# Masked maxima of an attention layer: ScalarE puts the mask into PSUM, and VectorE's mask and norm work is reordered

## What is computed

```
query = _layernorm(q @ Wq + bq, qn_scale, qn_bias)
key = _layernorm(kv @ Wk + bk, kn_scale, kn_bias)
...
scores = jnp.einsum('bhqd,bhkd->bhqk', query, key) / jnp.sqrt(jnp.asarray(D_K, query.dtype))
m = mask[:, None, :, :]
scores = jnp.where(m == 0, NEG_INF, scores)
probs = jax.nn.softmax(scores, axis=-1)
out = jnp.einsum('bhqk,bhkd->bhqd', probs, value)
...
x = x + jnp.tanh(g_xattn[1]) * _L1_xattn_ref(ctx_1024, _layernorm(x, axis=-1), mask_BxSxS2_ik0, ...)
```

## Time and profile before

| | us |
|---|---|
| median of 3 runs | 2475.44 (2474.05 to 2477.65) |
| span of the profiled execution, first to last instruction | 2475.2 |
| TensorE busy in it | 2414.1 |
| VectorE busy | 1444.5 |
| ScalarE busy | 1087.0 |

### The profile page before, as it was taken

How to read it: one execution, slowest core, us unless ns; L and a number is a source line. 1 busy time by engine, 2 the same in 40 slices (tenths; PEclk the granted TensorE clock), 3 DMA queues, 4 the chain that set the end, 5 groups by cost and what they waited for, 6 DMA issues and landing times.

```text
span 2475.2 us, 33128 instructions
## 1 busy us (share of the span) xinstructions
PE 2414.1 (98%) x13344; PEld 1826.1 (74%) x13344; DVE 1444.5 (58%) x2410; ACT 1087.0 (44%) x1762; POOL 245.9 (10%) x223
## 2 busy tenths in 40 slices
PE   6999999999999999999989999999999999999998
PEld 5666667688888888888755666666778888888886
DVE  5555566542222222222666666665888888888986
ACT  4343433442222222223334333334666666666665
POOL 2021112210000000000301111112000000000000
PEclk9999999999999999999999999999999999999999
DMA  3121111421101100102311222223501101101000
GB/s 126 35 86 52 52 52 69 158 85 52 52 1 52 51 18 35 51 18 85 113 58 61 78 78 78 78 73 102 167 18 35 52 18 48 38 20 49 35 30 22
DMA packets 92600, 147.27 MB, mean 59 GB/s; under 512 B 5408, under 2 KB 28320, under 8 KB 92448
## 3 DMA queue, kind: packets, MB, share of 16 engines
q1 hardware_dynamic: 92448, 145.16, 17.4%
HBM read 111.59 MB, written 33.55 MB: 59 GB/s over the span
## 4 chain that ended last, share of the span: by engine, by line
PE 40%; DVE 8%; ACT 2%; issue 1%; DMA 0%; POOL 0%; SPq 0%; DVEq 0%; ACTq 0%
PE l_lay_bank L69 18%; PE l_lay_score L69 11%; PE l_lay_values L1493 1%; PE l_lay_score L1416 1%; PE l_lay_score L1418 1%; PE l_lay_score L1468 1%; PE l_lay_values L1497 1%; PE l_lay_sums L1505 1%; DVE l_at_at_next L1036 1%; DVE l_at_h_lo L1050 1%; DVE l_at_at_next L1029 1%; DVE l_at_full L1025 1%; DVE l_at_full L1018 1%; DVE l_at_xTf_lo L924 1%; PE l_lay_bank L1339 1%
## 5 line engine op out<-in xcount | busy, mean ns | idle before, releaser
L69 PE MATMUL l_lay_score<-l_at_tw_hi,l_at_h_hi 128*128 128x512 f32 x1024 | 401.5, 392 | 5.2 <-DVE l_at_h_lo L1050 4.7
L69 PE MATMUL l_lay_bank<-l_at_xTf_hi,l_at_tw_hi 128*128 128x512 f32 x1024 | 400.0, 391 | 0.0
L69 PE MATMUL l_lay_score<-l_at_tw_hi,l_at_h_lo 128*128 128x512 f32 x1024 | 398.7, 389 | 0.0
L69 PE MATMUL l_lay_score<-l_at_tw_lo,l_at_h_hi 128*128 128x512 f32 x1024 | 398.5, 389 | 0.0
L69 PE MATMUL l_lay_bank<-l_at_xTf_hi,l_at_tw_lo 128*128 128x512 f32 x1024 | 398.4, 389 | 0.0
L69 PE MATMUL l_lay_bank<-l_at_xTf_lo,l_at_tw_hi 128*128 128x512 f32 x1024 | 398.4, 389 | 0.0
L1010 DVE TENSOR_TENSOR l_at_h_lo<-l_at_full,l_at_h_hi 128x512 fp32r<-128x512 f32 x128 | 99.6, 779 | 466.0 <-ACT l_at_h_hi L740 466.0
L735 ACT ACTIVATE l_at_full<-l_lay_bank,l_at_lay_b 128x512 f32<-128x512 f32 x128 | 88.4, 690 | 457.5 <-PE l_lay_bank L69 457.5
L69 PEld LDWEIGHTS l_lay_score<-l_at_tw_hi,l_at_h_hi 128*128 128x128 f32 x1024 | 192.2, 188 | 49.2 <-DVE l_at_h_lo L1050 10.3
L69 PEld LDWEIGHTS l_lay_score<-l_at_tw_hi,l_at_h_lo 128*128 128x128 f32 x1024 | 192.2, 188 | 40.3
L69 PEld LDWEIGHTS l_lay_bank<-l_at_xTf_hi,l_at_tw_lo 128*128 128x128 f32 x1024 | 192.2, 188 | 40.0
(11 more groups left out here) (224 smaller groups left out, 4078.9 us busy)
## 6 DMA issues: line engine op xcount, KB each, us to landing
both_x_in<-stream SPq DMA_DIRECT2D x25, 1024.0 KB, 5.6
l_at_xg<-stream SPq DMA_DIRECT2D x23, 1024.0 KB, 5.5
stream<-l_at_xg SPq DMA_DIRECT2D x22, 1024.0 KB, 4.3
l_at_tw_raw<-in_l_w SPq DMA_DIRECT2D x64, 256.0 KB, 5.6
l_at_maskT_in<-in_maskT SPq DMA_DIRECT2D x40, 256.0 KB, 2.6
both_x_in<-in_x SPq DMA_DIRECT2D x9, 1024.0 KB, 7.6
l_at_xg<-in_x SPq DMA_DIRECT2D x7, 1024.0 KB, 5.3
out<-l_at_xg SPq DMA_DIRECT2D x7, 1024.0 KB, 4.3
```

The source lines that it names most:

```text
L69: done = nc.tensor.matmul(out, lhs[a], rhs[b], start=first and n == 0, stop=last and n == len(passes) - 1)
```

## The change

ScalarE writes the mask into PSUM for maxima 4 to 15 of chunks 1 to 7 of layer 1 (`seed_max`), and TensorE's key product accumulates onto it. Maxima 0 to 3 and all of chunk 0 keep the identity product. From maximum 4 on three pairs of banks rotate, `values` and `sums` being the third. `seed_max` stands on ScalarE behind `s_evict`; its first one waits for `c_out` and `s_out`, the others for the reduction of maximum m - 3. On VectorE the four main pieces of the transposed mask move from among the maxima of chunk `it` to the start of the next turn of the loop, `mask_front` and x's norm move ahead, and one query piece moves. On SyncE pieces 3 and 4 are loaded at the head of the turn in which they are used.

```diff
@@ PSUM and the rotation
-        score = n.ps("score", [P, GH, 512])
-        values = n.ps("values", [P, 512])
-        sums = n.ps("sums", [P, 512])
+        score = n.ps("score", [P, GH + 2, 512])
+        values, sums = score[:, GH, :], score[:, GH + 1, :]
+        SEED0 = 4
+        N_SEED = NM - SEED0
+        pair_of = lambda it, m: m % 2 if it == 0 or m < SEED0 else (m - 2) % 3
+        pair_before = lambda m: m - 3 if m > SEED0 else None
+        max_banks = lambda it, m: score[:, 2 * pair_of(it, m):2 * pair_of(it, m) + 2, 0:2 * KEYS]
@@ SyncE, the loop over chunks
             for it in range(NCH):
+                if norm and it:
+                    load_maskT(it, 3)
+                    load_maskT(it, 4)
                 if it < last:
                     load(it + 2)
                 else:
                     load_last_residual()
-                if norm and it + 2 < NCH:
-                    load_masks(it + 2)
+                if norm and it:
+                    load_maskT(it + 1, 0)
+                    load_maskT(it + 1, 1)
                 if norm:
-                    for i in range(2, PIECES):
-                        load_maskT(it + 1, i)
-                    load_maskT(it + 2, 0)
-                    load_maskT(it + 2, 1)
+                    if it + 2 < NCH:
+                        load_masks(it + 2)
+                    load_maskT(it + 1, 2)
@@ ScalarE
+            def seed_max(it, m):
+                if m == SEED0:
+                    act.wait_ge(mask_done, it + 1)
+                    act.wait_ge(c_out, KT * it)
+                    act.wait_ge(s_out, it)
+                else:
+                    act.wait_ge(max_done, NM * it + pair_before(m) + 1)
+                nc.scalar.activation(max_banks(it, m).rearrange("p a (h k) -> p a h k", h=2),
+                                     mask_add[:, m % QT, :].unsqueeze(1).unsqueeze(1)
+                                     .broadcast_to([P, 2, 2, KEYS]), ACT.Copy).then_inc(seeded, 1)
...
                 s_evict(it)
+                if more and norm:
+                    for m in range(SEED0, NM):
+                        seed_max(it + 1, m)
@@ VectorE, the loop over chunks
-                xT_front(it + 1)
+                xT_front(it + 1, (0, 1))
+                if norm and it:
+                    maskT_front(it, 1)
+                    maskT_front(it, 2)
+                xT_front(it + 1, (2, 3))
...
                 if norm:
+                    if it:
+                        maskT_front(it, 3)
+                        maskT_front(it, 4)
+                    mask_front(it + 1)
+                    q_rows_front(it + 1, (0, 1))
+                    maskT_front(it + 1, 0)
+                    norm_stats(it + 2)
+                    q_rows_front(it + 1, (2,))
+                    norm_apply(it + 2)
+                    q_rows_front(it + 1, (3,))
                     q_norm_stats(it + 1)
+                    q_norm_apply(it + 1)
...
                 for m in range(NM):
                     max_of(it + 1, m)
-                    if m in (2, 3) and norm:
-                        qT_front(it + 1, (m,))
-                    if m in (4, 6, 10, 13) and norm:
-                        maskT_front(it + 1, {4: 1, 6: 2, 10: 3, 13: 4}[m])
+                    if m in (1, 3, 5) and norm:
+                        qT_front(it + 1, ((m + 1) // 2,))
@@ TensorE, max_of
-                if m >= 2:
+                if seed:
+                    pe.wait_ge(seeded, N_SEED * (it - 1) + m - SEED0 + 1)
+                elif m >= 2:
                     pe.wait_ge(max_done, NM * it + m - 1)
...
-                    if norm:
+                    if norm and not seed:
                         nc.tensor.matmul(to, ident_bf[:, :], mask_add[:, q, :].unsqueeze(1)
                                          .broadcast_to([P, 2, KEYS]), start=True, stop=False)
                     done = nc.tensor.matmul(to, qT_of(it)[0][:, t, q * P:(q + 1) * P],
                                             keys.bd[:, b, t, 2 * a:2 * a + 2, :],
-                                            start=not norm, stop=True)
+                                            start=not norm, stop=True, skip_group_check=seed)
```

More of the change, by code:

```diff
@@ L590, in _ @@
                     add_bias(last, gate_bias)
+                if it < last:
+                    x_rstd_of(it + 2)
                 if norm and it < last:
                     q_rstd_of(it + 1)
-                if it < last:
-                    x_rstd_of(it + 2)
                 if it:
@@ L967, in max_of @@
                 dve.wait_ge(max_ps, NM * it + m + 1)
-                heads = score[:, 2 * (m % 2):2 * (m % 2) + 2, 0:2 * KEYS]\
-                    .rearrange("p a (h k) -> p a h k", h=2)
+                heads = max_banks(it if norm else 0, m).rearrange("p a (h k) -> p a h k", h=2)
                 to = maxes[:, q, :].rearrange("p (j c) -> p j c", c=DH)[:, :, t]
@@ L1189, in _ @@
                     k_lo_of(1)
-                for half in ((0, 1), (2, 3)):
-                    if norm:
[L1192 to L1196, removed]
-                if norm:
+                if norm:
+                    if it:
[8 more added lines that the diff above has]
+                    q_rows_front(it + 1, (3,))
                     q_norm_stats(it + 1)
-                    norm_stats(it + 2)
                     q_norm_apply(it + 1)
                 else:
+                    q_front(it + 1, (0, 1))
+                    norm_stats(it + 2)
+                    q_front(it + 1, (2, 3))
                     norm_apply(it + 2)
@@ L1205, in _ @@
                 if norm:
-                    mask_front(it + 1)
-                    maskT_front(it + 1, 0)
-                    norm_apply(it + 2)
-                    qT_front(it + 1, (0, 1))
+                    qT_front(it + 1, (0,))
                 if it:
@@ L1226, in _ @@
                     front.take_lo(dve, "wd")
-            xT_front(NCH)
+            xT_front(NCH, (0, 1))
+            if norm:
+                maskT_front(last, 1)
+                maskT_front(last, 2)
+            xT_front(NCH, (2, 3))
             recip_of(last - 1)
+            if norm:
+                maskT_front(last, 3)
+                maskT_front(last, 4)
             for u in range(2):
@@ L1400, in max_of @@
                 t, q, b = m // QT, m % QT, it // CPB
+                seed = norm and it > 0 and m >= SEED0
                 if m == 0 and norm:
@@ L1413, in max_of @@
                 for a in range(2):
-                    to = score[:, 2 * (m % 2) + a, 0:2 * KEYS].rearrange("p (h k) -> p h k", h=2)
-                    if norm:
+                    to = max_banks(it if norm else 0, m)[:, a, :].rearrange("p (h k) -> p h k", h=2)
+                    if norm and not seed:
                         nc.tensor.matmul(to, ident_bf[:, :], mask_add[:, q, :].unsqueeze(1)
```

1 line of the change is left out of this document (added).

## The result

The changed kernel takes 2523.22 us (2522.25 to 2528.7, 4 runs), the kernel before on the same chip 2474.74 us (2473.79 to 2477.65, 4 runs). The ratio is 1.0194, with a 95% interval of 1.0181 to 1.0207: slower, by 48.5 us, where 5.2 had been forecast. The profiled execution has a span of 2526.9 us.

The account below looks back on a forecast made before the run. TensorE's own work was taken to bound the maxima of chunks 2 to 7. Maxima -14.3, late mask pieces +11.2 (chunks 2 to 7) and +5.9 (chunk 1), clock +2.4: +5.2 us, giving 2480.6 us; range 2468 to 2489.

Parts of the forecast that it names:

- the train and its feeder: Maxima 4 to 15, chunks 2 to 7: 0.98 us a step, ScalarE's mask 0.7 us, 1.1 us lost before maximum 4.
- the new order: Norm work reordered on VectorE and GpSimd: fills VectorE's own gaps, put at 0.
- The term of -14.3 us: Maxima of chunks 2 to 7: 3.5 us won less 1.1 lost in each of six chunks, 14.3 us gained.
- the landing: Mask pieces 3 and 4 behind the residual's load: land 7.1 us after its issue, TensorE goes on after 7.6.
- the stores: Stores ahead of the residual's load: 4.36 us each gives 9.6 us of stops, this trace's durations 13.0; 11.2 taken.
- I take 7.1: Time from the large load's issue until a mask piece behind it lands: 7.1 us, bounded below by 3.6.
- the forecast's faster rival: Mask pieces ready 4.1 us after the residual's issue; only chunk 1 stops, for 2.4 us; -12 us, 2463.5; chance 0.16.
- Its conversion, 0.42 us: VectorE's conversion of a late mask piece before the scores' mask products: 0.42 us, within the 7.6 until TensorE goes on.
- one fall for sure and half of another: 2.4 us: TensorE's clock behind the stops: one certain fall of 1.7 us and half of another, 2.4 us in all.
- a stop of 1.6 us is probably free of it: TensorE's clock: probably no fall after a 1.6 us stop; 5.9 us is not free, 3 us may not be.
- Chunk 1, put at 0: Chunk 1's maxima: no gain or loss, 0 (-1 to +1), the 2.3 us loop being as long as its three reductions.

Follow-up runs that it names:

- e8: Kernel before with only the changed order of norm, mask and qT on VectorE and of rstd on GpSimd; no ScalarE masks, mask pieces unmoved: 2477.08 us.
- e4: Changed kernel plus one wait: GpSimd's addition of the gate's bias starts only after VectorE has converted the chunk's mask pieces: 2493.48 us.
- e9: Changed kernel with mask pieces 3 and 4, from the second chunk on, converted by ScalarE and not VectorE; GpSimd's addition unchanged: 2494.18 us.
- e6: Changed kernel with unread products added on TensorE just ahead of the products that wait for the mask pieces, filling the stops: 2513.32 us.
- e1: Changed kernel with the mask pieces' loads and conversions back in their old places; ScalarE's masks and the new order kept: 2465.95 us.
- e2: Kernel before with only the mask pieces' loads and conversions (and the conversion for the maxima) moved; no ScalarE masks: 2539.01 us.
- e7: Changed kernel with the residual's load behind pieces 3 and 4, and ScalarE's eviction of the sums and first mask moved ahead: 2457.22 us.
- e10: Changed kernel with mask pieces in their old places, and ScalarE's eviction of the sums and first mask moved ahead: 2458.95 us.

## Why the prediction was right or wrong

*Right: the train and its feeder.* 0.98 us a step, 0.69 for the mask, 1.08 in front of maximum 4, and nothing from the new order (e8). The term of -14.3 us measured -12.8 (2.1 us a chunk against 2.4: maximum 4 starts 2.50 us after maximum 3 where it was 1.26, so the start costs 1.2, and the train gives back 3.4).

*Right: the landing; too low: the stores.* "I take 7.1" for a piece behind the large load, and 7.6 until TensorE goes on: in e4, where GpSimd waits, piece 4 was converted 6.9 to 7.0 us after the residual's issue in five of the seven chunks, and TensorE went on after 7.3 to 7.5. In chunk 3 it was 7.6 and 8.0 us (1457.22 to 1464.78 and 1465.26), in chunk 1 8.2 and 8.7. The stops of e4 add up to 21.2 us against 17.1. Of these 4.1 us, 1.1 are chunk 1's later landing. The other 3.0 are the stores: three of the six took 6.0 to 6.2 us, which makes 14.2 us of stops in chunks 2 to 7, where the prediction took 11.2 and had 13.0 from the stores of its own trace. The piece's 2.6 us, on which the forecast's faster rival stood (the median of all 40), didn't hold in this company. The Trainium skill's fit (DMA: Bandwidth & Descriptors, Anatomy of one DMA) is stated there for DMAs issued by GpSimd, where these are SyncE's; the 5.6 us estimated from it for 1.5 MB are 1.3 us short of the 6.9 measured.

*Wrong: "Its conversion, 0.42 us".* The row was read where GpSimd is idle. The step moved the conversion to just behind the landing of the residual's load, and that landing starts GpSimd's 4.5 us addition. The prediction costed the load that stands ahead of the piece in the queue, and did not ask what else its landing releases. The conversion pair takes 4.48 us where 0.84 was allowed, and in chunk 7, with two additions, 8.81. The stops fell from 47.1 to 21.2 us when GpSimd was made to wait: 25.9 us of the error.

*Wrong: "one fall for sure and half of another: 2.4 us".* The guess that a stop of 1.6 us is probably free of it held for most (e4: 1.63 kept the clock, 1.97 lost it; e9: 1.65, 1.69 and 1.71 kept it, 1.66 lost it). The price of a fall was near: 1.4 us each by the medians of e6 and 1.7 to 2.8 in the profiled execution, against the 1.7 that the rows gave. But every stop was 4.8 us or longer, so the clock fell seven times, for 9.9 us by the medians. The count failed, and it failed because the length of the stops had.

*The sum again:* 2465.95 (e1) + 47.1 + 9.9 = 2522.95, measured 2523.22. In spans of the profiled executions it is 2463.5 + 47.1 + 15.7 = 2526.3, measured 2526.9. Of the +43.3 us that the forecast lacked, 25.9 are the conversion, 4.1 the landing and the stores, 7.5 the clock by the medians, and 2.7 the gain in the maxima and chunk 1. The rest, some 3 us, is no part of the kernel that these runs can show: the kernel before itself had medians of 2474.74 and 2477.1 us in two sets. Chunk 1, put at 0, costs 1.2: its maxima now run at 0.50 of the clock, behind the wait of 2.67 us for ScalarE's mask. The clock stays at 1.00 there in e2 and e8, which have no such masks, and falls in e7 and e10 too, where the longest of these waits is 1.3 us. What brings it down there was not tried.

## What to carry to other kernels

When an instruction is moved behind a transfer, look up who else starts when that transfer or its neighbour in the queue lands, and whether that engine can hold yours: here one GpSimd instruction held VectorE's conversion for as long as it lasted. A duration from the trace holds for the company in which it was measured. A small transfer that something waits for belongs ahead of the large one that nothing waits for yet: one moved line was worth 59 us here, and then the change was 13 us faster than the kernel before, about as much as with the pieces left in their old places (e1, 11 us).

## What the runs showed of the hardware

- VectorE's conversion of 128x512 from int32 to bf16 takes 0.42 us alone; two of them took 4.48 to 4.52 us behind the start of one GpSimd addition of 128x2048 f32, and 8.81 us behind two (changed kernel). ScalarE did the same work in 0.63 us each, in the middle of such an addition, which took 4.55 us as against 4.50 (e9).
- ScalarE writes 128x616 f32 of a broadcast bf16 mask into PSUM in 0.69 us, and the key products accumulate onto it (changed kernel; products had written these banks before).
- A pair of 256 KB loads behind 1 MB on the same queue reached VectorE 6.2 to 6.5 and 6.9 to 7.6 us after the large one's issue in chunks 2 to 7 of e4.
- Behind a stop of 4.8 us the granted clock was 0.50 for 5 to 6 us of work (changed kernel, chunk 2); the same stop filled with products left it at 1.00 (e6).
- Stops of 1.63, 1.65, 1.69 and 1.71 us left it at 1.00, stops of 1.66, 1.95 and 1.97 us were followed by 0.50 to 0.53 (e4, e9).
